# Four graph layers on one core: the relation layer's sums per node by mask products on TensorE instead of a running sum on VectorE

## What is computed

```
h   = einsum('nd,rdo->rno', x, W_rel)          # 8 relations
msg = h[edge_type, src]                        # one row of 128 for each edge
agg = segment_sum(msg, dst, num_segments=n)
deg = maximum(segment_sum(ones, dst, n), 1)
out = relu(x @ W_self_w.T + W_self_b + agg / deg)
```

## Time and profile before

| What | Value |
|---|---|
| Median of three runs | 8349.12 us |
| The profiled execution's own time | 8378.33 us |
| Its span, first to last instruction | 8376.5 us |
| Mean granted TensorE clock | 0.532 of full speed |
| Instructions | 30,090 |

### The profile page before, as it was taken

The page is one execution under the profiler, slowest core; times in us unless marked ns, Lnnn a source line. Parts: engine busy times, 40 slices in busy tenths (PEclk is TensorE's granted clock), DMA queues, the critical chain, the costliest instruction groups (busy, mean ns, idle before and its releaser), DMA issues.

```text
span 8376.5 us, 30090 instructions
## 1 busy us (share of the span) xinstructions
PE 583.0 (7%) x2254; PEld 405.5 (5%) x2254; DVE 3873.6 (46%) x13120; ACT 976.0 (12%) x2890; POOL 5693.2 (68%) x5446
## 2 busy tenths in 40 slices
PE   1100000000000420000000000016700000000000
PEld 1100000000000320000000000013400000000000
DVE  6344554455545635555555555577422222222223
ACT  1121221122211120000000000055300000000000
POOL 4566666666765557777777777585277777777775
PEclk7555555555555655555555555558855555555555
DMA  4255555555655213333333333323432322322322
GB/s 161 81 170 186 179 194 171 187 185 181 209 170 182 60 58 98 99 99 98 99 99 100 99 94 99 97 61 110 188 97 88 95 94 92 97 92 92 97 92 87
DMA packets 293303, 1013.00 MB, mean 121 GB/s; under 512 B 103056, under 2 KB 120080, under 8 KB 230240
## 3 DMA queue, kind: packets, MB, share of 16 engines
q1 hardware_dynamic: 114192, 638.77, 20.1%
q0 software_dynamic: 175872, 369.49, 17.5%
q10 hardware_dynamic: 3024, 2.82, 0.1%
HBM read 511.47 MB, written 499.22 MB: 121 GB/s over the span
## 4 chain that ended last, share of the span: by engine, by line
DVE 28%; POOL 15%; issue 10%; another core or an unknown queue 6%; PE 3%; DMA 1%; POOLq 0%; ACT 0%; DVEq 0%; ACTq 0%; SPq 0%
DVE edge_rows L1770 19%; POOL edge_rows L849 12%; DVE edge_rows L995 3%; DVE old L989 2%; POOL node_sums L1050 2%; PE ps L1620 2%; POOL edge_rows L1719 1%; PE ps L1607 1%; DVE edge_rows L971 0%; DVE stats L1304 0%; PE ps L1661 0%; DVE edge_rows L942 0%; DMA edge_rows<-table_b,src_i 0%; DVE run_max L935 0%
## 5 line engine op out<-in xcount | busy, mean ns | idle before, releaser
L1719 POOL DMA_INDIRECT edge_rows<-table_rel,rel_row x1568 | 1650.2, 1052 | 645.3 <-issue 518.9
L849 POOL DMA_INDIRECT edge_rows<-table_b,src_i x1568 | 1662.5, 1060 | 618.0 <-issue 474.2
L849 POOL DMA_INDIRECT edge_rows<-table_a,src_i x1568 | 1563.8, 997 | 734.7 <-issue 470.2
L1770 DVE SCALAR_TENSOR_TENSOR edge_rows<-edge_rows,keep 128x128 f32<-128x128 f32 x1567 | 554.5, 354 | 1628.2 <-DVE edge_rows L1770 1097.1
L986 DVE SCALAR_TENSOR_TENSOR edge_rows<-edge_rows,weight_decay 128x129 f32<-128x129 f32 x1567 | 546.9, 349 | 307.8 <-DVE attrs L1011 179.5
L1011 DVE SCALAR_TENSOR_TENSOR attrs<-attrs,keep 128x128 f32<-128x128 f32 x1567 | 544.0, 347 | 303.7 <-DVE edge_rows L986 168.6
L995 DVE TENSOR_TENSOR edge_rows<-edge_rows,old 128x132 f32<-128x132 f32 x1567 | 460.4, 294 | 381.6 <-remote 149.1
L989 DVE TENSOR_TENSOR old<-edge_rows,weight_decay 128x132 f32<-128x132 f32 x1567 | 459.1, 293 | 351.8 <-remote 179.7
L894 ACT ACTIVATE weight_decay<-weight_decay 128x32 f32<-128x32 f32 (+1 forms) x196 | 52.8, 269 | 4027.5 <-remote 1435.1
L902 ACT ACTIVATE edge_rows<-edge_rows,weight_decay 128x129 f32<-128x129 f32 x1568 | 470.1, 389 | 3.2
L917 DVE TENSOR_TENSOR z<-edge_rows,dst_logit 128x16 f32<-128x16 f32 (+1 forms) x196 | 39.2, 200 | 472.8 <-DMA edge_rows<-table_b,src_i 258.6
(11 more groups left out here) (293 smaller groups left out, 3000.9 us busy)
## 6 DMA issues: line engine op xcount, KB each, us to landing
sums_b<-edge_rows SPq DMA_DIRECT2D x98, 1120.0 KB
sums_a<-edge_rows SPq DMA_DIRECT2D x98, 1040.0 KB
attrs<-in_ea SPq DMA_DIRECT2D x98, 1024.0 KB
sums_attr<-attrs SPq DMA_DIRECT2D x98, 1024.0 KB
sums_rel<-edge_rows SPq DMA_DIRECT2D x98, 1024.0 KB
table_rel<-rel SPq DMA_DIRECT2D x98, 512.0 KB
edge_rows<-table_a,src_i POOLq DMA_INDIRECT x1568
edge_rows<-table_b,src_i POOLq DMA_INDIRECT x1568
```

Source lines behind the costliest of these rows:

```text
L849: e.indirect_dma_start(out=rows[:, s, c, :], out_offset=None, in_=L.table, in_offset=bass.IndirectOffsetOnAxis(ap=src[:, g * GC + c:g * GC ...
L1719: e.indirect_dma_start(out=rows[:, s, c, :], out_offset=None, in_=table_rel, in_offset=bass.IndirectOffsetOnAxis(ap=rel_row[:, g * GC + c: ...
L1770: i = e.scalar_tensor_tensor(rows[:, s, c, :], before, keep[:, g * GC + c:g * GC + c + 1], rows[:, s, c, :], ALU.mult, ALU.add)
```

## The change

The relation sweep lays the edges out the other way: column t of the 128 partitions holds the 128 consecutive edges of tile t. For each tile TensorE multiplies a 128x128 mask with the tile's rows. Entry (p, i) of the mask is 1 where i is the place of the first edge in this tile that has the destination of edge p, so row i of the product is that node's sum within the tile. A second product with a single column (`is_last`) takes the sum of the tile's last node. The masks are made on VectorE, four tiles at a time, by comparing 0..127 (`place_bank`, kept in PSUM) with `first_of` (SBUF). ScalarE copies four products at a time back to the rows' buffer, over the rows that were fetched, and SyncE stores the group as before.

A node whose edges cross a tile's border is mended by batches of 112 tiles, 14 in all (`Carry`): a scan over the last nodes' sums gives what comes into each tile, a transposition turns it, and it is added to row 0 of the tiles that go on, which SyncE loads again from memory and stores back. The steps of a batch are spread over the groups behind it (`due`).

The tables for this (`first_of`, `carry_keep`, `is_last`, `goes_on`, `tile_row`) are made in the graph stage and three of them are kept in device memory until the sweep. Further edits: `keep` no longer lives past the attention layers, the sweep's crossing is gone, GpSimd's wait for the sums is gone, the node stage fetches by `tile_row`, and many semaphores are shared between stages under common names.

```diff
@@ graph_stage: sync, scalar
+            for i, at in enumerate((first_of, carry_keep, is_last)):
+                e.wait_ge(*first_put.at(i + 1))
+                e.dma_start(first_dram[i], at[:, :]).then_inc(first_saved.sem, 16)
+            e.wait_ge(*first_saved.at(48))
...
+            e.dma_start(before_i[0:TB, :], io["dst_before"]).then_inc(tiles_loaded.sem, 16)
+            e.dma_start(rel_row[:, :], io["src_t"]).then_inc(edges_loaded.sem, 16)
+            e.wait_ge(*float_stored.at(16))
+            e.dma_start(tile_f[0:TB, :, :], dst_float.rearrange("a b -> (a b)").rearrange("(b p e) -> p b e", p=TB, e=P)
+                        ).then_inc(tiles_loaded.sem, 16)
...
+            for b in range(0, NB, 4):
+                n = min(4, NB - b) * TB
+                i = e.activation(first_of[:, b * TB:b * TB + n], ps[:, b // 4, 0:n], ACT.Copy)
+            i.then_inc(first_put.sem, 1)
...
@@ graph_stage: vector, edge_places
+                e.wait_ge(*tiles_loaded.at(32))
...
+                then(e.tensor_tensor(goes_on[0:TB, :], before[0:TB, :], tile_f[0:TB, :, 0], ALU.is_equal))
+                t = then(e.tensor_tensor(tile_cut[0:TB, :, 1:P], tile_f[0:TB, :, 1:P], tile_f[0:TB, :, 0:P - 1],
+                                         ALU.not_equal))
+                yield
...
+                t1 = then(e.tensor_tensor(tile_cut[0:TB, :, :], tile_cut[0:TB, :, :],
+                                          bc(place[0:TB, :].unsqueeze(1), [TB, NB, P]), ALU.mult))
+                t = then(e.memset(tile_f[0:TB, :, :], 1.0))
+                yield
...
+                e.tensor_tensor_scan(flat, tile_f[0:TB, :, :].rearrange("p b e -> p (b e)"), flat, 0.0,
+                                     ALU.mult, ALU.max).then_inc(first_known.sem, 1)
+                yield
...
+                e.tensor_tensor(turned_last[0:TB, :, :], turned_first[0:TB, :, :],
+                                bc(turned_first[0:TB, :, P - 1:P], [TB, NB, P]), ALU.is_equal).then_inc(alone_known.sem, 1)
...
@@ graph_stage: tensor
+            e.wait_ge(*table.copied.at(NK))
+            e.wait_ge(*first_known.at(1))
+            for b in range(NB):
+                i = e.transpose(ps[:, b // 4, (b % 4) * TB:(b % 4 + 1) * TB], turned_first[0:TB, b, :],
+                                ident[0:TB, 0:TB])
...
@@ Carry (new)
+        def v_sum(self, e, b):
...
+            e.tensor_tensor_scan(run[:, 1:TB + 1], self.carry_keep[:, b * TB:(b + 1) * TB], ps[:, self.bank(b), 0:TB],
+                                 before, ALU.mult, ALU.add).then_inc(self.summed.sem, 1)
...
+        def v_add(self, e, b):
+            at = self.first[0:TB, b % 2, :]
+            e.wait_ge(*self.taken.at(b + 1))
+            e.wait_ge(*self.first_loaded[b % 2].at(16 * (b // 2 + 1)))
+            e.tensor_tensor(at, at, self.before[0:TB, b % 2, :], ALU.add).then_inc(self.added.sem, 1)
...
@@ edges_rel_stage: gpsimd
                 if g >= NS:
                     e.wait_ge(*stored[s].at(16 * (g // NS)))
-                if g >= NS - 1:
-                    e.wait_ge(*summed.at(g - NS + 2))
...
@@ edges_rel_stage: sync
+                e.wait_ge(*moved.at((g + 1) * NQ))
+                e.dma_start(groups_of(sums_rel)[:, cols(g), :], rows[:, g % NS, :, :]).then_inc(stored[g % NS].sem, 16)
+                for b in carry.due(g, NS):
+                    for k in range(g - 2 * NS + 1, g - NS + 1):
+                        e.wait_ge(*stored[k % NS].at(16 * (k // NS + 1)))
+                    carry.q_first(e, b)
+                for b in carry.due(g, NS + 4):
+                    carry.q_store(e, b)
...
@@ edges_rel_stage: scalar
+                    e.wait_ge(*summed.at(n + 1))
+                    e.activation(rows[:, g % NS, q * QC:(q + 1) * QC, :].rearrange("p c d -> p (c d)"),
+                                 ps[:, n % NO, 0:QC * D], ACT.Copy).then_inc(moved.sem, 1)
...
@@ edges_rel_stage: tensor
+                e.wait_ge(*gathered[g % NS].at(16 * GC * (g // NS + 1)))
+                for q in range(NQ):
+                    n = g * NQ + q
+                    for c in range(q * QC, (q + 1) * QC):
+                        t = g * GC + c
+                        done = e.matmul(carry.last_at(t), rows[:, g % NS, c, :], is_last[:, t:t + 1], start=True,
+                                        stop=True)
...
+                    e.wait_ge(*masked.at(n + 1))
+                    if n >= NO:
+                        e.wait_ge(*moved.at(n - NO + 1))
+                    for c in range(QC):
+                        done = e.matmul(ps[:, n % NO, c * D:(c + 1) * D], masks[:, n % NM, c, :],
+                                        rows[:, g % NS, q * QC + c, :], start=True, stop=True)
+                    done.then_inc(summed.sem, 1)
...
@@ edges_rel_stage: vector
-                    i = e.scalar_tensor_tensor(rows[:, s, c, :], before, keep[:, g * GC + c:g * GC + c + 1],
-                                               rows[:, s, c, :], ALU.mult, ALU.add)
...
+                for q in range(NQ):
+                    n = g * NQ + q
+                    if n >= NM:
+                        e.wait_ge(*summed.at(n - NM + 1))
+                    e.tensor_tensor(masks[:, n % NM, :, :], bc(place_bank.unsqueeze(1), [P, QC, P]),
+                                    bc(first_of[:, n * QC:(n + 1) * QC].unsqueeze(2), [P, QC, P]), ALU.is_equal
+                                    ).then_inc(masked.sem, 1)
...
@@ nodes_rel_stage
-        sums = NodeSums("node_sums", sb, sums_rel, D, 3)
+        sums = NodeSums("node_sums", sb, sums_rel, D, 3, tile_row)
```

More of the change, by code:

```diff
@@ L27, in padded_sizes, with batch_of_tiles @@
     return nj, ec
+def batch_of_tiles(ec):
+    return max(d for d in range(GC, P + 1, GC) if ec % d == 0)
 def chunk_len(ep):
@@ L156, in build @@
     cut = sb_edges("cut", [P, EC])
+    keep = sb_edges("keep", [P, EC])
     stage_done = sem("stage_done")
@@ L542, in vector @@
             then(e.memset(ones[:, :], 1.0))
-            e.wait_ge(*counted_off.at(3))
+            e.wait_ge(*counted_off.at(4))
+            then(e.tensor_copy(place[:, :], place_i[:, :]))
             then(e.tensor_scalar(ident[:, :], col_i[:, :], 0.0, None, ALU.is_equal))
@@ L1039, in build, with __init__ @@
     class NodeSums:
[L1042 to L1043 removed]
+        def __init__(self, name, sb, sums, W, depth=2, row=sum_row):
+            self.sums, self.depth, self.row = sums, depth, row
             self.buf = sb(name, [P, depth, JB, W])
@@ L1350, in nodes_b_stage @@
         rel = sb("rel", [P, NSR, NREL, D])
-        rel_stored = [sem(f"rel_stored{i}") for i in range(NSR)]
+        rel_stored = [sem_of(f"rows_stored{i}", 16 * turns(NJ, NSR, i)) for i in range(NSR)]
         nodes = AttentionNodes(B, sb, node_b, lambda k: out_b[:, k % 3, :, :])
@@ L1737, in scalar @@
             e.dma_start(b_self[:, :], io["d_self_b"].broadcast_to([P, D])).then_inc(self_loaded.sem, 16)
+            e.activation(place_bank, place[:, :], ACT.Copy).then_inc(places_put.sem, 1)
+            for g in range(NG):
+                for q in range(NQ):
[3 more added lines that the diff above has]
+                                 ps[:, n % NO, 0:QC * D], ACT.Copy).then_inc(moved.sem, 1)
@@ L1739, in tensor @@
         def tensor(e):
             e.wait_ge(*self_loaded.at(32))
-            for i, j0 in enumerate(own_blocks):
-                if i >= 2:
-                    e.wait_ge(*own_added.at(i - 1))
-                for j in range(j0, min(j0 + 4, NJ)):
-                    done = e.matmul(ps[:, 6 + i % 2, (j - j0) * P:(j - j0 + 1) * P], own_part[:, j, :], w_self[:, :],
-                                    start=True, stop=True)
-                done.then_inc(own_product.sem, 1)
-            crossing.tensor(e)
+            e.wait_ge(*last_loaded.at(32))
@@ L1783, in nodes_rel_stage @@
         sb = buffers(local)
-        sums = NodeSums("node_sums", sb, sums_rel, D, 3)
-        out_ready = sem("out_ready")
-        out_stored = [sem(f"out_stored{i}") for i in range(3)]
+        sums = NodeSums("node_sums", sb, sums_rel, D, 3, tile_row)
+        out_ready = sem_of("x_ready", NK)
+        out_stored = [sem_of(f"rows_stored{i}", 16 * turns(NK, 3, i)) for i in range(3)]
         def gpsimd(e):
```

271 lines of the change are left out of this document (220 added, 51 removed).

## The result

The changed kernel takes 8747.18 us (median of four runs, 8718.52 to 8770.79); the kernel before, beside it, 8344.62. The ratio is 1.048, 95% interval 1.044 to 1.052: slower by 403 us, where I had forecast 218 us less. The profiled run of the changed kernel is its fastest, 8718.52 us.

What follows compares the result with a forecast made beforehand. POOL's issue of 1568 gathers was taken to bound the sweep, slowed by DVE's sums. Gathers -209, tail -19 and graph stage +10 gave -218 us: 8131 us from the median of 8349, range 8090 to 8230.

Steps and rivals of the forecast that it cites:

- POOL's pace: Relation sweep: with the chained sums gone, gathers keep 1.25 us each, 1960 us against 2169, a gain of 209 us.
- over 96 gathers no backlog: Sweep's start: gathers at 1.255 us, landing 2.59 us after issue both times; argued against the pace staying at 1.40.
- PE hides behind POOL: Relation sweep: PE's products take 12.6 us a group (10.8 to 14.6), hidden under 20.0 us of gathers.
- The sign that I named for it: Relation sweep: PE takes about 12 to 13 us a group, then waits for the DMA.
- Masks and copies: Relation sweep: DVE masks 0.674 us, ACT copies 0.598 us, four each a group; masks cost POOL 0, copies hidden.
- rival 2: Relation sweep: masks take the sums' place in slowing POOL, 22.7 us a group, +47 us, 8396 us; chance 0.05.
- Tail: Last gather's end to first node fetch: 28 us instead of 46.8, gain 19 us (14 to 24).
- Graph stage: Making the new tables in the graph stage adds 10 us (2 to 25), PE and ACT work hidden.
- The third: Relation sweep: PE becomes the bound, eight waits a group stretched by 1.05 us, 23 us a group, 8434 us; chance 0.04.
- The first: Relation sweep: gathers stay at 1.40 us because POOL's full queue is slow by itself; 8364 us, no change; chance 0.12.

Runs made afterwards that it cites:

- the run with the long pause: Changed kernel with a 128x256 memset on POOL after each gather, gathers 1.44 us apart: 8425 us, ratio 1.011 to the kernel before.

## Why the prediction was wrong

**POOL's pace** (-209 us). This step failed: "I take it that a sum with two SBUF inputs and a gather's descriptor work shut each other out." They don't. With the lag and 15 of 16 sums gone the pace is 1.40 us all the same, and in the batch without the lag it is 1.25 with all sums, where taking them away is worth 11 us, not 209. I had the rows for it: DVE's beat after POOL was done is a queue that empties, and I read it so, but took the sums for its cause. (The beat is even only to 8199; from there to 8212 the sums start 0.70 to 2.10 us apart, the grid on which PE crawls now.) The argument against the right answer, "over 96 gathers no backlog", rested on landings, which don't show the lag: in the run with one sum a group the eleventh group's last gather was issued at 6198.46, after 219 us without a pause and shortly before the turn at 6213, and DVE had its rows 2.60 us later; in the first group it was 2.65. The backlog does not stand between a gather and its data. It stands between the other engines and their next instruction. The Trainium skill (SBUF — State Buffer, Who interferes with whom) has two SBUF inputs contend only with a GpSimd instruction that reads SBUF, and infers that a tensor_tensor does not hold up descriptor generation. These two runs agree with that inference, here for sums by scalar_tensor_tensor beside gathers; none of them has a GpSimd instruction whose reads of SBUF could be told apart.

The changed kernel does issue its gathers at 0.94 + 0.30 = 1.25 us, so the number of that step came true and its gain did not: the pace had been the lag's, and the lag stayed. In the two profiled runs the gathers, waits included, went from 2169 us to 2541: +372 in the place of -209.

**PE hides behind POOL.** This step failed too, and it is the one that makes the kernel slower. The size of the products was right: I had 12.6 us a group (10.8 to 14.6), and it is 13.65 undisturbed. The sign that I named for it did not appear, since PE does not wait for rows but crawls. The cost of a held instruction was in no term of the sum, though DVE's 1.05 us of idle before each sum was in the rows; I had kept it for waits. It holds for instructions that wait for nothing too, as ACT's 1200 show, and PE has eight records where DVE had one sum. Where the lag is there: no gathers, 14.0 us a group (1372 / 98); gathers at 1.44 us, 23.1 (the gathers' own); gathers at 1.25 us, 26.8 (2625 / 98).

**Masks and copies.** 0.687 and 0.597 us against 0.674 and 0.598, and the gathers beside them stay at 0.94 us: right, and rival 2 is out.

**Tail.** 83 us instead of 28, against 46.8 before: +36, not -19. When PE is not behind it is 29: from the last gather's end at 8223.4 to 8252.7 in the run with the long pause, from 7501.5 to 7530.9 where there is no lag. So the size of the term was right without the crawl; but without the lag the kernel before needs 20.7 us (7503.6 to its first node fetch at 7524.3), not 46.8, and the change loses 9 instead of gaining 19.

**Graph stage** (+10 us, "2 to 25"). With the lag 373.6 against 379.1 us to the first gather of the next stage, no cost that can be told; without it 337.7 against 328.0, so 9.7 us. That gives the sum without the lag: 10 for the graph stage, -11 for the gathers, +9 for the tail and -1 in between are 7 us, and the two spans are 7672.7 and 7666.1.

**Rivals.** The third, PE becomes the bound, came nearest: right in what ends last, wrong in the place of the price (eight waits a group at 1.05 us, where it is every instruction, at 0.70 to 2.80) and so in its size, 8434 against 8747. I had given it 0.04. The first was right about the pace, "POOL's queue is slow by itself once it is full", and wrong that this leaves the change at 8364: it took for granted that a slow queue is of no concern to an engine with eight times the instructions. The range was not the plain sum of its parts either: they give 8101 to 8244, where I had 8095 to 8220; nothing hangs on that.

**What stays open.** What it is that takes 1.40 us a gather cannot be seen in the trace. It hangs on the number of gathers, or on that of their packets, which was 32 for each with 128 rows and with 64; it does not make their data late; it holds ACT, DVE and PE alike; and it is there in the runs of the result and in four of the six batches, but not in the other two. Whether the chip, the machine around it or something that changes with time makes that difference, these runs don't tell: the numbers of the chips differ from batch to batch, but one came up twice, once with the lag and once without, and the two batches without it followed one another. Something that each instruction has to hand over, and of which every gather hands over a fixed amount, fits all of that, but it is a guess; whether the recording of the runs is such a thing was not tried. Where the turning point lies, between 1.395 and 1.442 us, is open too. No complete version here beats the kernel before in either condition: at 1.40 us a gather the gathers alone are 1568 x 1.40 = 2195 us (2169 in the kernel before, which is let ahead), and at 1.25 both have 1960.

## What to carry to other kernels

An idle time of "issue" on an even grid (0.70, 1.40, 2.10 us) that is the same for engines with no data in common is not that engine's own: before work moves to another engine, count its instructions, not only its busy time, beside the DMAs that are issued in the same stretch. A pace that changes after some number of DMAs (171 to 187 here), with the same work beside them before and after, suggests something behind the issuer that has filled up; one run without the suspected neighbour tells whether the neighbour is the cause. And where a time hangs on such a grid, compare in more than one batch: the difference between these two kernels is 403 us with the lag and 6 without.

## What was not expected of the hardware

- Beside 1568 gathers in a row, 1200 independent activations of 0.2 us took 1590 us (5957.7 to 7547.9): 51 at 0.093 us, then one for each gather of 1.40.
- A gather of 64 rows costs the other engines as much as one of 128, with as many packets: 8747 us both.
- Gathers 15% slower (1.44 us instead of 1.25) made the kernel 322 us faster, 8425 against 8747; at 1.395 us it was 204.
- The kernel before differed by 8% between batches, 8335 and 7668 us, at nearly the same granted clock (0.53 and 0.54 over the whole), and the ratio of two kernels went with it, from 1.048 to 1.001.
